# Routed experts of a mixture on their own tokens, by scatter and gather, instead of on all tokens

## Chip, cores and metric

One core of one Trainium2 chip. The metric is the time of one execution in device microseconds (us), as the median of several runs. A profile is one execution with the hardware profiler on.

## What is computed

Four residual layers on x of (2, 512, 256); each adds the layer norm of a block's output to x. The first three (a recurrent time mixing, an expert-choice layer, a delta-rule attention) are not touched by the change. The fourth is a mixture with a shared part and 8 routed experts of which each token takes 2:

```python
g = x @ sw1.T
u = x @ sw2.T
shared_out = jax.nn.silu(g) * u @ sw3.T            # 1024 hidden
scores = jax.nn.sigmoid(x @ router_w.T)            # 8 experts
_, top_idx = jax.lax.top_k(scores + expert_bias, TOPK)   # TOPK = 2
top_scores = jnp.take_along_axis(scores, top_idx, axis=-1)
top_scores = top_scores / (top_scores.sum(-1, keepdims=True) + 1e-09)
combine = jnp.zeros((T, E), x.dtype).at[jnp.arange(T)[:, None], flat_idx].add(flat_sc)
h12 = jnp.einsum('td,ehd->teh', flat_x, w12)       # 2 x 128 hidden per expert
h1, h2 = jnp.split(h12, 2, axis=-1)
out_e = jnp.einsum('teh,edh->ted', jax.nn.silu(h1) * h2, w3)
routed_out = jnp.einsum('ted,te->td', out_e, combine)
return shared_out + routed_out
```

## The kernel before

`sandwich` runs four stages one after the other, each a block in which the five engines have their own queues and meet through semaphores. The last is `expert_mixture`. Tokens are 1024 = 8 tiles of 128 (`NT`), 4 tiles to a batch (`TB`), a batch is 512 columns (`T`), and the 256 features are 2 chunks (`C`). The order of work on each engine is the order in which its function issues instructions; nothing moves them.

In the last stage the hidden units of the shared part (8 groups of 128, `SH`) and the 8 experts (128 hidden units each) are treated alike: 16 groups (`HID`), for each of 2 batches, so 32 steps (`STEPS`). Every expert is computed for every token and its hidden rows are scaled by the token's share for that expert, zero for those not chosen.

All products use operands split into a high and a low part (`HI`, `LO`), and three of the four products of parts (`PRODUCTS`). In step n TensorE does `up(n)`: for the gate and for the up weight 6 products of 512 columns (2 chunks x 3). ScalarE takes `silu(n)` of the gate, VectorE multiplies with the up half, GpSimd scales by the share where the group is an expert (L2243), ScalarE casts the high part (`high`, L2190), GpSimd subtracts for the low part (L2249), and three steps later (`LAG`) TensorE does `down(n)`: 12 products of 256 columns (L2135), which accumulate over the 16 groups in PSUM banks 0 and 1.

At the stage's head ScalarE and VectorE normalize x into xm, TensorE turns xm (L2090) into PSUM, the two engines split the turned rows (L2169, L2271) and ScalarE copies them once more (L2173) for the exact scores (L2098, after the first up product). VectorE chooses the two experts and makes the shares (`choose`, `weigh`) between the first steps, TensorE turns the shares (`turn_shares`, L2105), and they go to memory and back, spread over all partitions (L2220, L2226). The weights come turned from an earlier stage and are split, two groups of four 128 x 128 tiles per step, by ScalarE (`high_weights`, L2159) and VectorE (`low_weights`, L2262) in the first 14 steps. The first batch's sums are kept, normalized and added to x between the second batch's steps; the second batch's at the end (L2367, L296, L253, L2196, L2317), and x is stored (L2231).

```python
for n in range(STEPS + LAG):
    if n < STEPS:
        up(n)
    if n == SCORE_STEP:
        score()
    if n == SHARE_STEP:
        turn_shares()
    if n >= LAG:
        down(n - LAG)
```

## Time and profile before

| what | us |
|---|---|
| median of 3 runs (lowest, highest) | 476.74 (476.24, 477.44) |
| the profiled execution | 476.85 |
| its span, first to last instruction | 475.1 |
| TensorE busy in the span | 367.0 (77%) |
| VectorE, ScalarE, GpSimd busy | 294.2, 254.9, 122.4 |
| last stage, from its first instruction | 319.24 to 475.1 |

The difference between the execution's own time and its span, 1.75 us, lies before the first and after the last instruction. PE is TensorE's products, PEld its weight loads, which overlap them; DVE is VectorE, ACT ScalarE, POOL GpSimd, SP the queue that issues plain transfers. A q behind an engine's name is its queue (the sequencer). A duration of a TensorE product overlaps the next one's; how fast they follow one another is read from the chain or from the first and last of a run. The granted clock (PEclk) is a share of 2.4 GHz, 0.50 being 1.2 GHz.

### The profile page before, as it was taken

To read this page: it belongs to the slowest core of one execution; us is meant where nothing else is said; L and a number is where in the kernel's file an instruction comes from. 1 tells how busy PE (TensorE), PEld (TensorE's weight loads), DVE (VectorE), ACT (ScalarE), POOL (GpSimd) and SP (SyncE) were. 2 spreads that over 40 slices of the span, in tenths; PEclk is the share of its full clock that TensorE was granted. 3 is DMA by queue.
4 is the path that set the end of the run, shared out by engine and by line. 5 is a ranking of instruction groups with operands and counts; after the bars stand their busy time and mean duration, and the time that the engine had idled before them with its cause. 6 is when DMAs were issued, how large, how long until landed. Compare 5 with 4: busy or idle time off the path is not lost. (4 is left out here: it accounts for less than half of the span.)

```text
span 475.1 us, 10071 instructions
## 1 busy us (share of the span) xinstructions
PE 367.0 (77%) x4130; PEld 291.6 (61%) x4130; DVE 294.2 (62%) x622; ACT 254.9 (54%) x471; POOL 122.4 (26%) x148
## 2 busy tenths in 40 slices
PE   2999778866699766522158898846999999999993
PEld 1544567765477655311156455636888888888883
DVE  5799997796436565999973567784584211422223
ACT  2889774475457775582332457648745333354323
POOL 5393001400000015000017200030233665323661
PEclk9999989897999999555558959996899999999998
DMA  7790000000000000000000000000014500000001
GB/s 220 246 351 20 0 0 1 2 0 0 0 3 3 1 3 1 1 0 1 0 0 4 4 3 5 3 1 1 0 36 146 178 0 1 0 2 15 31 1 44
DMA packets 12489, 15.82 MB, mean 33 GB/s; under 512 B 2046, under 2 KB 10644, under 8 KB 12444
## 3 DMA queue, kind: packets, MB, share of 16 engines
q1 hardware_dynamic: 12444, 15.18, 10.2%
q8 instruction: 33, 0.54, 0.5%
q14 instruction: 12, 0.10, 0.1%
HBM read 14.09 MB, written 1.08 MB: 32 GB/s over the span
## 5 line engine op out<-in xcount | busy, mean ns | idle before, releaser
L2328 DVE TENSOR_TENSOR third<-third,ps 128x512 f32<-128x512 f32 x32 | 22.0, 686 | 81.7 <-PE ps L2119 67.7
L2249 POOL TENSOR_TENSOR hidden_r<-third,hidden_r 128x512 fp32r<-128x512 f32 x31 | 41.2, 1329 | 89.3 <-ACT hidden_r L2190 89.3
L2135 PEld LDWEIGHTS ps<-down_r,hidden_r 128*128 128x128 f32 x384 | 49.2, 188 | 3.2 <-POOL hidden_r L2249 0.9
L2135 PE MATMUL ps<-down_r,hidden_r 128*128 128x256 f32 x384 | 50.2, 280 | 0.7 <-POOL hidden_r L2249 0.7
L2119 PE MATMUL ps<-xm_r,gate_r 128*128 128x512 f32 x192 | 50.2, 398 | 0.0
L2190 ACT CAST hidden_r<-third 128x512 fp32r<-128x512 f32 x32 | 19.9, 623 | 56.4 <-PE ps L2135 56.4
L2119 PE MATMUL ps<-xm_r,up_r 128*128 128x512 f32 x192 | 50.0, 397 | 0.0
L2119 PEld LDWEIGHTS ps<-xm_r,up_r 128*128 128x128 f32 x192 | 36.9, 192 | 7.8
L1509 PE MATMUL ps<-ident,area 128*128 128x128 f32 x32 | 8.4, 414 | 40.4 <-DVE area L1839 40.4
L2119 PEld LDWEIGHTS ps<-xm_r,gate_r 128*128 128x128 f32 x192 | 34.8, 192 | 5.9 <-issue 0.2
L1509 PEld LDWEIGHTS ps<-ident,area 128*128 128x128 f32 x32 | 5.5, 207 | 43.2 <-DVE area L1839 43.2
L1836 DVE TENSOR_TENSOR third<-area 128x124 f32<-128x124 f32 (+15 forms) x31 | 29.2, 943 | 1.1
L2179 ACT ACTIVATE third<-ps 128x512 f32<-128x512 f32 x32 | 19.2, 599 | 19.4 <-PE ps L2119 19.4
L1839 DVE TENSOR_TENSOR area<-area,third 128x124 f32<-128x124 f32 (+15 forms) x31 | 27.9, 900 | 1.1
L1681 ACT ACTIVATE area<-ps,own_side 128x512 f32<-128x512 f32 (+1 forms) x16 | 15.9, 1100 | 19.9 <-PE ps L1509 19.9
L1737 ACT COPY area<-third 32x128 f32<-32x128 f32 x64 | 18.9, 295 | 14.0 <-DVE third L1883 12.7
L1130 POOL TENSOR_SCALAR keys_by_head<-k_t,own_fourth 128x512 f32<-128x512 f32 x4 | 3.9, 987 | 81.8 <-ACT k_t L1275 81.8
L1162 PE MATMUL ps<-w_r,x_r 128*128 128x512 f32 x96 | 19.2, 349 | 3.6 <-DVE beta_rows L1355 2.1
L2243 POOL TENSOR_TENSOR third<-third,stored 128x512 f32<-128x512 f32 x15 | 19.3, 1290 | 0.0
L1162 PEld LDWEIGHTS ps<-w_r,x_r 128*128 128x128 f32 x96 | 14.9, 188 | 7.0 <-issue 3.5
L1180 PE MATMUL ps<-proj_rows,third 128*32 128x128 f32 x384 | 15.2, 285 | 4.4 <-ACT qkv L1301 3.6
L1582 PE MATMUL ps<-area,k_t 128*32 128x128 f32 x128 | 15.5, 335 | 1.8 <-DVE area L1892 0.7
(343 smaller groups left out, 838.1 us busy)
## 6 DMA issues: line engine op xcount, KB each, us to landing
stored<-share_dram SPq DMA_DIRECT2D x8, 512.0 KB, 5.9
stored<-in_L_ffn_sw_dram SPq DMA_DIRECT2D x3, 1024.0 KB
stored<-in_L_ffn_w_dram SPq DMA_DIRECT2D x1, 2048.0 KB
x<-L_attn_hidden_state_dram SPq DMA_DIRECT2D x4, 256.0 KB, 3.4
out_dram<-x SPq DMA_DIRECT2D x4, 256.0 KB, 2.2
w_nat<-in_L_attn_Wk_dram SPq DMA_DIRECT2D x1, 256.0 KB, 2.7
w_nat<-in_L_attn_Wv_dram SPq DMA_DIRECT2D x1, 256.0 KB, 2.9
w_nat<-in_L_attn_Wr_dram SPq DMA_DIRECT2D x1, 256.0 KB, 4.1
```

The costliest lines, as they stand in the source:

```text
L1162: last = nc.tensor.matmul(ps[:, bank, 0:cols.stop - cols.start], own, w_r[:, wp, ci, cols], start=i == 0, stop=i == len(passes) - 1)
L1681: last = a(spread_rows(r, count, side), rows, ACT.Copy, scale=core.own_side[:, side:side + 1])
L1737: nc.scalar.copy(u_place[strand[q], n % U_SLOTS, :, q, :], u[strand[q], n % U_KEPT].rearrange("p (h e) -> p h e", h=HH)) \
L1836: link(V.tensor_tensor(part, rows.unsqueeze(3).to_broadcast([P, below, G, j + 1]), inv[:, j, :, 0:j + 1].unsqueeze(1).to_broadcast([P, bel ...
L1839: last = V.tensor_tensor(inv[:, j + 1:, :, 0:j + 1], inv[:, j + 1:, :, 0:j + 1], part, ALU.subtract)
L2119: last = nc.tensor.matmul(ps[:, bank + which, :], w[:, wp, c, a, :], xm_r[:, xp, c, b * T:(b + 1) * T], start=i == 0, stop=i == C * len(PR ...
L2135: last = nc.tensor.matmul(ps[:, t // 2, t % 2 * D:(t % 2 + 1) * D], hidden_r[:, n % 2, hp, t * P:(t + 1) * P], down_r[:, wp, a, :], start= ...
L2179: a(gated[:, n % 2, :], ps[:, 4 + 2 * (n % 2), :], ACT.Silu).then_inc(silu_ready, 1)
L2190: nc.scalar.copy(hidden_r[:, n % 2, HI, :], hidden[:, n % 4, :]).then_inc(hidden_hi, 1)
L2243: nc.gpsimd.tensor_tensor(hidden[:, n % 4, :], hidden[:, n % 4, :], share[:, a - SH, b * T:(b + 1) * T], ALU.mult) \
L2249: nc.gpsimd.tensor_tensor(hidden_r[:, n % 2, LO, :], hidden[:, n % 4, :], hidden_r[:, n % 2, HI, :], ALU.subtract).then_inc(hidden_lo, 1)
L2328: V.tensor_tensor(hidden[:, n % 4, :], gated[:, n % 2, :], ps[:, 4 + 2 * (n % 2) + 1, :], ALU.mult) \
```

## The change

The shared part keeps its steps (now 16: 8 groups x 2 batches). Each expert sees the tokens that chose it. The 2 x 1024 token rows are put, sorted by expert, into tiles of 128 rows of which each belongs to one expert; 23 tiles (`SLOTS`) hold every possible division. VectorE finds each row's place (`choose`, `place_tokens`), with sums over tokens by two small products (`count`). GpSimd scatters the rows of xm to their places in memory by 16 indirect transfers, SP loads the rows back tile by tile, and after 9 shared steps (`EARLY`) TensorE goes over the 23 tiles: it turns the rows, reads the tile's expert number into a register (`own_expert`), does the up products with weights addressed by it (6 of 256 columns), turns the product's rows, and does the down products (3 of 256 columns). ScalarE and VectorE split what is turned. The results are stored to memory, GpSimd gathers each token's two result rows by 16 indirect transfers into `found`, and VectorE adds them, times the token's shares, to the shared part's sums (`combine`). The seven other shared steps stand between the tiles and the end.

Further: the row buffer in memory is filled with input rows at the kernel's start (`fill_rows`), constants 8 to 23 are added, the turning of the input no longer waits for ScalarE's splits, splits of weights are dealt out to 9 steps, the low part of hidden rows is VectorE's (`low`), and the first batch's norm moves from between the steps to the tail.

```diff
+        self.rows_dram, self.results_dram = (self.nc.dram_tensor(name, ((2 * NT + E - 1) * P, D), F32, kind="Internal").ap()
+                                              for name in ("rows_dram", "results_dram"))
...
+    def fill_rows(self, sp, rows):
+
+        sp.wait_ge(self.f_in, self.f_in_total)
+        for start in range(0, self.rows_dram.shape[0], N):
+            some = min(N, self.rows_dram.shape[0] - start)
+            sp.dma_start(self.rows_dram[start:start + some, :], rows[0:some, :]).then_inc(self.f_in, 16)
+            self.rows_filled += 16
...
+        for e in range(24):
...
-    HID = SH + E
+    SLOTS = 2 * NT + E - 1
+    STEPS, EARLY, LAG = B * SH, 9, 3
+    ROW_PARTS = (0, 2, NT)
+    RESULT_PARTS = ((0, 8), (8, 16), (16, 20), (20, SLOTS))
...
+        routed_up = sb("routed_up", [P, 2, C, E, 2 * P], F32R)
+        routed_down = sb("routed_down", [P, 2, E, D], F32R)
...
+        AHEAD, PER_STEP = 8, (0, 2, 2, 2, 2, 2, 2, 2, 2)
...
+        COMBINED = {STEPS - 4: (0, 1), STEPS - 3: (2, 3), STEPS - 1: (4,)}
...
-                    pe.wait_ge(xm_kept, B * C)
                     for t in range(NT):
+                        if t == 0:
+                            pe.wait_ge(xm_kept, ROUTER + C)
+                        if t == TB:
+                            pe.wait_ge(xm_lo_kept, KEPT_LO)
...
+                def count():
+
+                    pe.wait_ge(routed, CHOSEN)
+                    for k, weights in enumerate((core.ones[:], upto_own)):
+                        last = nc.tensor.matmul(ps[:, 2, k * NT * E:(k + 1) * NT * E], weights,
+                                                flat(both), start=k == 0, stop=k == 1,
+                                                skip_group_check=True)
+                    last.then_inc(scores_done, 1)
...
+                def own_expert(j):
+                    expert[j] = nc.tensor.value_load(owner[0:1, j:j + 1], min_val=0, max_val=E - 1)
+
+                def turn_rows(j):
+                    if j in ROW_PARTS:
+                        pe.wait_ge(rows_in[ROW_PARTS.index(j)], 16)
+                    if j == 0:
+                        pe.wait_ge(routed, OWNED)
+                    if j >= 2:
+                        pe.wait_ge(xm_lo_kept, KEPT_LO + j - 1)
+                    for c in range(C):
+                        last = nc.tensor.transpose(ps[:, 2 + j % 2, c * P:(c + 1) * P], rows[:, j, c * P:(c + 1) * P],
+                                                   ident[:])
+                    last.then_inc(xm_turned, 1)
+
+                def up_routed(j):
+                    pe.wait_ge(xm_lo_kept, KEPT_LO + j + 1)
+                    pe.wait_ge(prod_ready, tile(j - 2) if j >= 2 else shared(EARLY - 2 + j))
+                    if j == 0:
+                        pe.wait_ge(*kept(groups[-1]))
+                    for i, (c, wp, xp) in enumerate((c, *parts) for c in range(C) for parts in PRODUCTS):
+                        last = nc.tensor.matmul(ps[:, 4 + j % 2, 0:2 * P], rows_t[j % 2][:, xp, c],
+                                                routed_up[:, wp, c, bass.DynSlice(expert[j], 1), :], start=i == 0,
+                                                stop=i == C * len(PRODUCTS) - 1)
+                    last.then_inc(up_done, 1)
+
+                def turn_hidden(j):
+                    pe.wait_ge(prod_ready, tile(j))
+                    if j:
+                        pe.wait_ge(hidden_lo, tile(j - 1))
+                    nc.tensor.transpose(ps[:, 6, 0:P], routed_hidden[:, j % 3], ident[:]).then_inc(scores_done, 1)
+
+                def down_routed(j):
+                    pe.wait_ge(hidden_lo, tile(j))
+                    if j:
+                        pe.wait_ge(rows_kept, j)
+                    for i, (wp, hp) in enumerate(PRODUCTS):
+                        last = nc.tensor.matmul(ps[:, 7, 0:D], routed_t[j % 2][:, hp],
+                                                routed_down[:, wp, bass.DynSlice(expert[j], 1), :], start=i == 0,
+                                                stop=i == len(PRODUCTS) - 1)
+                    last.then_inc(down_done, 1)
...
+                for n in range(EARLY):
+                    up(n)
+                    if n == 0:
+                        score()
+                    if n == COUNT_STEP:
+                        count()
+                    if n >= LAG:
+                        down(n - LAG)
+                for n in range(EARLY - LAG, EARLY - 1):
+                    down(n)
+                for j in range(SLOTS + 2):
+                    if j < SLOTS:
+                        turn_rows(j)
+                        own_expert(j)
+                    if 1 <= j <= SLOTS:
+                        up_routed(j - 1)
+                    if j == 2:
+                        down(EARLY - 1)
+                    if j >= 3:
+                        turn_hidden(j - 3)
+                    if j >= 4:
+                        down_routed(j - 4)
+                up(EARLY)
+                turn_hidden(SLOTS - 1)
+                down_routed(SLOTS - 2)
+                down_routed(SLOTS - 1)
+                for n in range(EARLY + 1, STEPS + LAG):
                     if n < STEPS:
                         up(n)
-                    if n == SCORE_STEP:
-                        score()
-                    if n == SHARE_STEP:
-                        turn_shares()
-                    if n >= LAG:
+                    if n - LAG >= EARLY:
                         down(n - LAG)
...
+                def high_rows(j):
+                    act.wait_ge(xm_turned, ROUTER + TURNED + j + 1)
+                    nc.scalar.copy(rows_t[j % 2][:, HI], ps[:, 2 + j % 2, 0:D].rearrange("p (c f) -> p c f", c=C)) \
+                        .then_inc(xm_hi_kept, 1)
+
+                def silu_routed(j):
+                    act.wait_ge(up_done, up_tile(j))
+                    a(gated[:, j % 2, 0:P], ps[:, 4 + j % 2, 0:P], ACT.Silu).then_inc(silu_ready, 1)
+
+                def high_routed(j):
+                    act.wait_ge(scores_done, HIDDEN_TURNED + j + 1)
+                    nc.scalar.copy(routed_t[j % 2][:, HI], ps[:, 6, 0:P]).then_inc(hidden_hi, 1)
+
+                def keep_rows(j):
+                    act.wait_ge(down_done, tile(j))
+                    nc.scalar.copy(rows[:, j], ps[:, 7, 0:D]).then_inc(rows_kept, 1)
...
-                sp.wait_ge(share_t_kept, 1)
-                sp.dma_start(core.share_dram, share_t).then_inc(share_out, 16)
-                sp.wait_ge(share_out, 16)
-                for part in range(2):
-
-                    sp.wait_ge(kept_dve, quad_kept[2 * part + 1])
-                    for e in range(4 * part, 4 * part + 4):
-                        sp.dma_start(share[:, e, :], core.share_dram[e].partition_broadcast(P)) \
-                            .then_inc(share_in[part], 16)
+                sp.wait_ge(rows_out, 16 * 2 * NT)
+                for part, start in enumerate(ROW_PARTS):
+                    stop = (ROW_PARTS + (SLOTS,))[part + 1]
+                    sp.wait_ge(*kept(quads[1][-1] if part < 2 else groups[-1]))
+                    sp.dma_start(rows[:, start:stop], tiles(core.rows_dram)[:, start:stop, :]) \
+                        .then_inc(rows_in[part], 16)
+
+                for start, stop in RESULT_PARTS:
+                    sp.wait_ge(rows_kept, stop)
+                    sp.dma_start(tiles(core.results_dram)[:, start:stop, :], rows[:, start:stop]) \
+                        .then_inc(results_out, 16)
...
+                pool.wait_ge(core.f_in, core.f_in_total + core.rows_filled)
+                pool.wait_ge(routed, PLACED)
+                for t in range(NT):
+                    for k in range(2):
+                        nc.gpsimd.indirect_dma_start(core.rows_dram, bass.IndirectOffsetOnAxis(slots[:, k, t:t + 1], 0),
+                                                     xm[:, t, :], None).then_inc(rows_out, 16)
+                pool.wait_ge(results_out, 16 * (1 + len(RESULT_PARTS)))
+                for t in range(NT):
+                    for k in range(2):
+                        nc.gpsimd.indirect_dma_start(found[:, k, t, :], None, core.results_dram,
+                                                     bass.IndirectOffsetOnAxis(slots[:, k, t:t + 1], 0)) \
+                            .then_inc(results_in[t // 2], 16)
...
+                def place_tokens():
+
+                    dve.wait_ge(scores_done, 2)
+                    link(V.tensor_tensor_scan(flat(upto_tile), flat(not_first[:]), ps[:, 2, 0:NT * E], 0.0, ALU.mult,
+                                              ALU.add))
...
+                    V.tensor_copy(slots[:], slots_f[:]).then_inc(routed, 1)
...
+                def low(n):
+                    dve.wait_ge(hidden_hi, shared(n))
+                    V.tensor_tensor(hidden_r[:, n % 2, LO, :], hidden[:, n % 4, :], hidden_r[:, n % 2, HI, :],
+                                    ALU.subtract).then_inc(hidden_lo, 1)
...
+                def combine(t):
+
+                    if t % 2 == 0:
+                        dve.wait_ge(results_in[t // 2], 16 * 4)
+                    if t < TB:
+                        link(V.scalar_tensor_tensor(y[:, t], found[:, 0, t], share[:, 0, t:t + 1], y[:, t], ALU.mult,
+                                                    ALU.add))
+                    else:
+                        link(V.tensor_scalar(y[:, t], found[:, 0, t], share[:, 0, t:t + 1], None, ALU.mult))
+                    return V.scalar_tensor_tensor(y[:, t], found[:, 1, t], share[:, 1, t:t + 1], y[:, t], ALU.mult,
+                                                  ALU.add)
...
+                for n in range(4, AHEAD):
+                    low_weights(n)
+                dve.wait_ge(scores_done, 1)
+                for n in range(EARLY):
+                    product(n)
+                    if n == 0:
+                        choose()
+                    if n == PLACE_STEP:
+                        place_tokens()
+                    if n:
+                        low(n - 1)
+                    for k in groups_of(n):
+                        low_weights(k)
+                    if n == WEIGH_STEP:
+                        weigh()
+                low(EARLY - 1)
+                for j in range(SLOTS + 3):
+                    if j < SLOTS:
+                        low_rows(j)
+                    if 1 <= j <= SLOTS:
+                        product_routed(j - 1)
+                    if j == 1:
+                        keep_first()
+                    if j == SLOTS + 2:
+                        product(EARLY)
+                    if j >= 3:
+                        low_routed(j - 3)
+                for n in range(EARLY + 1, STEPS):
+                    product(n)
+                    low(n - 1)
+                    for t in COMBINED.get(n, ()):
+                        last = combine(t)
+                    if n == STEPS - 2:
+                        link(last)
+                        finish_first(0)
+                low(STEPS - 1)
+                finish_first(1)
+                for t in range(STEPS_COMBINED, NT):
+                    last = combine(t)
+                    if t == STEPS_COMBINED:
+                        finish_first(2)
+                link(last)
                 for t in range(TB):
                     if t % 2 == 0:
-                        dve.wait_ge(down_done, STEPS + t // 2)
-                    last = V.bn_stats(norm.stats[:, TB + t, :], summed(t))
+                        dve.wait_ge(down_done, shared(STEPS - 1) + t // 2)
+                    link(V.tensor_tensor(y[:, TB + t], y[:, TB + t], summed(t), ALU.add))
+                    last = norm.tile_stats(y, TB + t)
```

TensorE, an inner tile of the routed part in the changed kernel (stored holds the token rows and, transposed next, the hidden rows; owner the experts' numbers):

```order
L2220 MATMUL ps<-ident,stored 128x128 [waits xm_lo_kept]
L2220 MATMUL ps<-ident,stored 128x128
L2210 TENSOR_LOAD owner
L2210 ISA x2
L2230 ISA [waits prod_ready,xm_lo_kept]
L2230 MATMUL ps<-routed_up,xm_r 128x256 x2
L2230 ISA
L2230 MATMUL ps<-routed_up,xm_r 128x256
L2239 MATMUL ps<-ident,stored 128x128 [waits hidden_lo,prod_ready]
L2246 REGISTER_ALU [waits routed_rows_kept,hidden_lo]
L2246 MATMUL ps<-routed_down,xm_r 128x256 x2
```

Nothing of this is in the kernel before, whose queue there goes from one `up` to one `down` of 12 products each; register instructions stand between the products, and the first of a group carries its waits.

GpSimd in the last stage before (hidden_r the split hidden rows; third holds the hidden rows themselves):

```order
L2249 TENSOR_TENSOR hidden_r<-third,hidden_r 128x512 [waits hidden_hi] x2
L2249 TENSOR_TENSOR hidden_r<-third,hidden_r 128x512 [waits down_done,hidden_hi] x6
L2243 TENSOR_TENSOR third<-third,stored 128x512 [waits prod_ready,share_in_first]
L2249 TENSOR_TENSOR hidden_r<-third,hidden_r 128x512 [waits down_done,hidden_hi]
L2243 TENSOR_TENSOR third<-third,stored 128x512 [waits prod_ready,share_in_first]
```

and in the changed kernel (stored now holds `found`):

```order
L2395 MEMSET third 128x128
L2396 AFFINE_SELECT third<-third 128x128 [waits masks_order]
L2403 DMA rows_dram<-xm,slots 2944x256 [waits tokens_routed,f_in,masks_order]
L2403 DMA rows_dram<-xm,slots 2944x256 x15
L2408 DMA stored<-results_dram,slots 128x256 [waits rows_in_2]
L2408 DMA stored<-results_dram,slots 128x256 x15
```

The subtractions and scalings have gone from GpSimd (the subtractions to VectorE), and 32 indirect transfers have come.

VectorE at the end of the changed kernel (xm holds the sums, stored the gathered rows):

```order
L2498 TENSOR_TENSOR hidden_r<-third,hidden_r 128x512 [waits hidden_hi]
L313 RECIPROCAL ln_inverse_std<-ln_std_dev 128x4 [waits ln_std]
L278 SCALAR_TENSOR_TENSOR ln_shift<-ln_mean_var,ln_inverse_std 128x4 [waits dve_order]
L2535 TENSOR_SCALAR xm<-stored,share 128x256
L2536 SCALAR_TENSOR_TENSOR xm<-stored,share,xm 128x256 [waits dve_order]
L2548 SCALAR_TENSOR_TENSOR x<-xm,ln_inverse_std,x 128x256 [waits scores_kept] x4
L2535 TENSOR_SCALAR xm<-stored,share 128x256 [waits results_in_3]
L2536 SCALAR_TENSOR_TENSOR xm<-stored,share,xm 128x256 [waits dve_order]
L2535 TENSOR_SCALAR xm<-stored,share 128x256
L2536 SCALAR_TENSOR_TENSOR xm<-stored,share,xm 128x256 [waits dve_order]
L2608 TENSOR_TENSOR xm<-xm,ps 128x256 [waits down_done,dve_order]
L302 BN_STATS ln_stats<-xm 128x6 [waits dve_order]
```

Before, the last subtraction was followed by the four statistics straight from PSUM; now the first batch's roots and adds, three pairs of combining and a sum ahead of each statistic stand there.

## Rows read from the trace of the kernel before

**Rows 1.** Head of the page: span, busy time by engine, bytes moved in 40 slices.

```profile
span 475.1 us, 10071 instructions
...
PE 367.0 (77%) x4130; PEld 291.6 (61%) x4130; DVE 294.2 (62%) x622; ACT 254.9 (54%) x471; POOL 122.4 (26%) x148
...
GB/s 220 246 351 20 0 0 1 2 0 0 0 3 3 1 3 1 1 0 1 0 0 4 4 3 5 3 1 1 0 36 146 178 0 1 0 2 15 31 1 44
```

**Rows 2.** Chain of waits that ended last, in time: start us, us, what.

```profile
320.02 2.07 ACT xm L272 x4
...
324.29 3.68 PE ps L2090 x16
327.96 3.39 PE ps L2119 x12
331.35 3.47 PE ps L2098 x32
...
348.89 0.97 PE ps L2105 x8
...
366.45 1.41 PE ps L2135 x12
367.86 2.73 PE ps L2119 x12
...
465.19 2.42 PE ps L2135 x18
467.62 0.02 issue
467.64 1.48 DVE ln_stats L2367 x4
...
470.84 1.68 DVE x L2317 x4
```

**Rows 3.** Stretches: us, busy PE, PEld, DVE, ACT, POOL, granted clock, DMA share, GB/s.

```profile
324.30:328.00 3.70, 3.70 (x17) 3.54 (x18) 2.45 (x5) 1.76 (x3) 0.00 (x0) 0.50 0.00 0
380.00:420.00 40.00, 40.00 (x231) 35.27 (x230) 9.20 (x21) 12.23 (x20) 19.08 (x15) 1.00 0.00 1
200.00:250.00 50.00, 16.39 (x275) 13.36 (x262) 45.34 (x48) 21.05 (x25) 1.80 (x3) 0.53 0.00 0
```

**Rows 4.** Timeline of TensorE, 68 to 76 us: turns of weight tiles.

```profile
72.17 2.78 PE L129 MATMUL ps<-ident,stored 128*128 128x128 f32 x24
```

**Rows 5.** Timeline of SP's queue, 0 to 60 us: issues of small transfers.

```profile
4.70 0.25 SPq L383 DMA_DIRECT2D vec_rows<-urrent_token_weight_dram  x1
...
12.91 3.71 SPq L166 DMA_DIRECT2D onorm<-in_L_attn_onorm_w_dram  x8
```

**Rows 6.** Groups by shape, 315 to 476 us: busy us, mean ns | idle before.

```profile
L2249 POOL TENSOR_TENSOR hidden_r<-third,hidden_r 128x512 fp32r<-128x512 f32 x31 | 41.2, 1329 | 89.3 <-ACT hidden_r L2190 89.3
...
L2190 ACT CAST hidden_r<-third 128x512 fp32r<-128x512 f32 x32 | 19.9, 623 | 56.4 <-PE ps L2135 56.4
...
L2262 DVE TENSOR_TENSOR down_r<-stored,down_r 128x512 fp32r<-128x512 f32 x8 | 5.4, 686 | 0.1
...
L2306 DVE COPY xm<-ps 128x256 f32<-128x256 f32 x4 | 1.4, 417 | 4.8 <-PE ps L2135 4.8
...
L2292 DVE TENSOR_TENSOR first<-first,scores 128x64 f32<-128x64 f32 x1 | 0.2, 226 | 0.0
```

**Rows 7.** Transfers: line, count, KB each, median us from issue to landing.

```profile
out_dram<-x SPq DMA_DIRECT2D x4, 256.0 KB, 2.2
...
onorm<-in_L_attn_onorm_w_dram SPq DMA_DIRECT2D x8, 0.1 KB, 2.6
```

**Rows 8.** Timeline of GpSimd, 0 to 130 us; in brackets idle before and releaser.

```profile
1.81 1.20 POOL L178 MEMSET numbers<- 128x1 f32 x8
...
18.48 1.86 POOL L199 TENSOR_SCALAR third<-third,conv_w 128x131 f32<-128x131 f32 x3 [9.59 <-DMA onorm<-in_L_attn_onorm_w_dram]
```

379 lines of the change are left out of this document (212 added, 167 removed).

## The prediction

> **What bounds the kernel now.** I read the head of the page first, then the chain of waits over the last stage, then that stage by stretches, and last the groups of instructions by shape. The span is 475.1 us of 476.85 us for the profiled execution; the median of the runs shown is 476.74, so the two may stand for one another. The changed stage is the last one, from about 319 us. Its chain consists almost entirely of TensorE [rows 2]: 12 products of 512 columns take 2.73 us and 12 of 256 take 1.41, so a step of up and down products costs 4.14 us, and there are 32 of them (2 batches of 16 groups). Between 380 and 420 us TensorE is busy without a gap at the full granted clock [rows 3]. VectorE, ScalarE and GpSimd wait for it there. So the time is TensorE's queue, and a change pays as far as it shortens that queue without putting a wait in it.
>
> **The change, part by part.** *Removed steps.* The 8 routed experts are no longer computed for every token: 16 of the 32 steps go. 16 x 4.14 = **-66.2 us** [rows 2], on the path entirely.
>
> *Added tiles.* 23 tiles of 128 token rows come instead. Each has 2 turns of its rows, 6 up products of 256 columns, 1 turn of its hidden rows and 3 down products of 256 columns. A product of 256 is 1.41/12 = 0.118 us [rows 2]; a turn at full clock 2.78/24 = 0.116 us [rows 4]. The array's share is 9 x 0.118 + 3 x 0.116 = 1.41 us. Besides, TensorE's queue has to read the tile's expert number from SBUF into a register (TENSOR_LOAD) and run eight register instructions, which the trace of before nowhere shows. Below: nothing, if the queue runs ahead of the array. Above: each of the nine at the shortest instruction which the trace shows a queue carrying out itself, a transfer's issue of 0.25 us [rows 5], which makes 1.41 + 2.25 = 3.66. The load is the one that reaches out to memory, so I price it like one of SP's small issues, 3.71/8 = 0.46 us [rows 5]. The register instructions touch nothing outside the queue; I take 0.02 us each, the gap that the chain of waits calls "issue" [rows 2], 0.16 together. Some of the load is behind waits on a semaphore, so I don't hide it: 2.03 us per tile, 23 x 2.03 = **+46.7 us** (32.4 to 84.2). The Trainium skill (DMA: Bandwidth & Descriptors, Latency and other measured facts) gives about 600 ns as the floor of a `tensor_load`; by that, as an estimate, a tile would be 2.17 and the sum 3.2 us higher. No run here shows it.
>
> The other engines of a tile fit under 2.03 us: ScalarE reads 256 columns twice and 128 twice. A 512-column cast takes 0.62 and VectorE's 256-column copy 0.42 [rows 6]; with 0.42 and 0.3, twice each, that is 1.44 us, and VectorE's three reads are 0.42 + 2 x 0.3 = 1.02. Within an iteration each turned bank is read before it is needed again one iteration later. Filling and draining this pipeline (first tile's turn, cast, subtraction; last tile's mirror image; the four copies of the first batch's sums on VectorE at the second tile) is some 0.12 + 0.42 + 0.42 at each end plus hand-overs: **+2.5 us** (1 to 5).
>
> *Head.* The turning of the input now starts when two rows of a batch are there instead of behind ScalarE's eight copies and splits: before, the turns run from 324.29 at 0.23 us each, at half clock, and the first up product at 327.96 [rows 2, 3]. Now they can start near 321.1, so the first batch is turned near 323, and with two casts, two subtractions and the first weights the product starts near 325.7. The scores hang on copies of the turned rows as before, so they end about 2.0 us earlier. The eight turns of the shares, 0.97 us [rows 2], go. New on the path: two small sums (count) that wait for VectorE's choice. Choice is a product (0.69) and 20 small instructions; they end about 3.9 us after the scores, while the up product between lasts about 3.7, so count costs about 0.6. Then 15 linked small instructions (0.23 each [rows 6]) stand on VectorE ahead of the third product, which comes about 0.4 us late. Sum: -2.0 - 0.97 + 0.6 + 0.4 = **-2.0 us** (-4 to +2). From then on VectorE has a product, a subtraction that was GpSimd's (1.33 there, 0.69 here [rows 6]) and two weight splits per step: 4 x 0.69 = 2.76, under the step's 4.14.
>
> *Scatter and gather.* GpSimd issues 16 indirect transfers of 128 rows, then 16 back. The trace has none. Below: 0.46 us each, SP's issue. Above: each waiting for the one ahead to land, 0.46 + 2.6 [rows 5, 7]. I take 1.33, what GpSimd's own 128-row instructions take [rows 6], for it is that engine which prepares them. Places known near 340.9, the first tile wanted near 368.7 (after 9 up and 8 down steps): 27.8 us, less a landing (2.6) and the load of the first two tiles (2.2 [rows 7]) leaves 23, so up to 1.43 us each costs nothing. On the way back the last pair is wanted 28 us after the last tile; less the store (2.6) and a landing (2.6), again 1.42 each. **0 us** at 1.33 (21.3), with the seven remaining shared steps as cover; without that cover it would be the whole 21.
>
> *Tail.* Before, from the last product's end to the span's end: 475.1 - 467.6 = 7.5 us [rows 1, 2]. Now VectorE has behind its last subtraction (about 1.8 us before the products end) the first batch's roots, one linked pair to combine, four adds (0.42 each at the spacing of [rows 2], 1.68/4), two more pairs (0.9 each), then four sums with a linked statistic (0.85 each) where there were four statistics alone (1.48). That puts the statistics' end about 6.9 us behind the products instead of 1.5: **+5.4 us** (2 to 8). The wait of 0.3 us net at the last down product of before goes: **-0.3**.
>
> Covered and free: 16 more constants on GpSimd's queue at 1.20/8 = 0.15 us, 2.4 in all, ahead of a wait of 9.59 us for a transfer [rows 8]; if that wait were gone they'd cost 2.4. Three fills of the row buffer (3 MB) on SP's queue behind the weights, when the transfers are idle from 40 us on [rows 1]; SP has nothing else until the last stage.
>
> Sum: -66.2 + 46.7 + 2.5 - 2.0 + 0 + 5.4 - 0.3 = -13.9. **476.85 - 13.9 = 463 us.** The tile's price breaks even at 2.03 + 13.9/23 = 2.63 us.
>
> **The rivals.**
> *A, GpSimd's transfers become the bound (slower).* If each of the 32 has to wait out one VectorE instruction of 0.69 us, it takes 2.02 us. Then the scatter is 16 x (2.02 - 1.43) = 9.4 us late at the first tile, and the gather 16 x (2.02 - 1.42) = 9.6 at the last pairs: 463 + 19 = 482. It decides against the change from 1.43 + 13.9/32 = 1.86 us each. For it: VectorE is two thirds busy where the scatter runs; against: no row shows GpSimd and VectorE holding each other up in this stage, its 1.28 to 1.33 hold throughout. The Trainium skill (SBUF — State Buffer, SBUF: two separate sides) says that VectorE in a two-port mode locks GpSimd out of the port through which it writes descriptors, so such a transfer waits for VectorE's instruction; nothing here shows it.
> *B, the clock falls in the tiles.* The granted clock is 0.50 while the input is turned after a pause, and 0.53 between 200 and 250 us, where TensorE is busy a third of the time [rows 3]. At 1.2 GHz a tile is 9 x 0.236 + 3 x 0.23 = 2.81 us: 463 + 23 x 0.78 = 481. For it: gaps in every tile; against: the array would still be busy 70%.
> *C, the queue runs ahead.* The loads lie wholly under the array's work, 1.41 us per tile: 463 - 14.3 = 449.
> That the change does not do what it says is no rival: the order of instructions shows the tiles and the loads.
>
> **How the numbers follow.** Forecast 0.53, A 0.20, B 0.10, C 0.17. About 0.3% (1.4 us) is what a measurement of this kernel can tell from no change. The forecast's own range is 455 to 474 (tile 1.7 to 2.5 us); a twentieth of all lies near break-even, and a part of the forecast goes over it through the load's upper bound: faster 0.66, same 0.05, slower 0.29. The range goes from C to beyond A and B: 447 to 486; the upper bound of nine full issues (500) is left out.
>
> **What would show it.** A tile's period in the routed part: 2.0 us says the load is paid, 1.4 that it is hidden, 2.8 with a granted clock of 0.5 says B. GpSimd's indirect transfers 1.3 us apart, and no wait of the first turned rows for their load, say the scatter is covered; a TensorE wait of some 10 us there says A. The statistics' end about 7 us behind the last product confirms the tail. I am wrong if a tile costs over 2.6 us at full clock, or if a transfer that no row of before shows stands between the shared steps and the tiles.

## The result: 475.5 us, a ratio of 0.991, where 463 us was forecast

The changed kernel takes 475.51 us (median of 20 runs, 470.23 to 489.35), the kernel before 477.76 us beside it (20 runs, 474.8 to 484.5). The ratio is 0.9906 with a 95% interval of 0.9881 to 0.9931: faster by about 1%. The forecast was faster by 2.9% (463.0 of 476.74 us). So the sign was right and the time lies in the range of 447 to 486, but only about a third of the gain that was worked out came (0.94% of 2.9%). The profiled execution took 470.29 us, its span 468.2 us; it is one of the fastest. Medians here and below count every execution, while ratios leave out those in a slower state that some executions of every kernel fall into.

The head of the page of the changed kernel, beside [rows 1], with the software queue that the indirect transfers use:

```profile
span 468.2 us, 10194 instructions
...
PE 345.0 (74%) x4018; PEld 270.8 (58%) x4018; DVE 322.6 (69%) x730; ACT 256.0 (55%) x527; POOL 101.4 (22%) x152
...
PEclk9999989897999997755559959997899789999986
...
q0 software_dynamic: 1536, 4.20, 2.8%
```

TensorE has 22 us less work than in [rows 1], and the span is 6.9 us shorter. The other 15 us have become time in which TensorE stands. TensorE's timeline shows where (start, busy time, line, operation, output and inputs, count, in brackets the idle time ahead and what ended it; the lines chosen are the landmarks of the last stage):

```profile
325.88 1.66 PE L2182 MATMUL ps<-xm_r,gate_r 128*128 128x512 f32 x6 [0.35 <-DVE xm_r L2430]
...
363.96 0.60 PE L2198 MATMUL ps<-down_r,hidden_r 128*128 128x256 f32 x3 [0.42 <-issue]
366.07 0.40 PE L2198 MATMUL ps<-down_r,hidden_r 128*128 128x256 f32 x2 [1.51 <-issue]
366.80 0.52 PE L2198 MATMUL ps<-down_r,hidden_r 128*128 128x256 f32 x1 [0.33 <-issue]
367.50 1.45 PE L2198 MATMUL ps<-down_r,hidden_r 128*128 128x256 f32 x6 [0.18 <-issue]
369.38 5.03 PE L2198 MATMUL ps<-down_r,hidden_r 128*128 128x256 f32 x24 [0.44 <-DVE hidden_r L2498]
374.26 0.60 PE L2220 MATMUL ps<-ident,stored 128*128 128x128 f32 x4
...
420.67 1.62 PE L2182 MATMUL ps<-xm_r,gate_r 128*128 128x512 f32 x6
...
453.17 5.49 PE L2198 MATMUL ps<-down_r,hidden_r 128*128 128x256 f32 x24 [3.39 <-DVE hidden_r L2498]
```

The first up product comes 2.1 us earlier than in [rows 2] (325.88, not 327.96), as forecast. Then one down product, 12 matmuls with no wait between them, takes from 363.96 to 368.95 us where it took 1.41 [rows 2], and "issue" says that the profile shows nothing which TensorE waited for. The next two products take 5.03 us where two of 1.41 are 2.82, and the first turned rows (L2220) come at 374.26, not at 368.7 as worked out. Ahead of the last two down products TensorE stands 3.39 us, and they take 5.49. ScalarE's timeline, and behind it some lines of VectorE's, show that these two stood as well:

```profile
353.89 0.60 ACT L2309 ACTIVATE third<-ps 128x512 f32<-128x512 f32 x1 [0.71 <-PE ps L2182]
354.39 1.13 ACT L2288 CAST routed_up<-stored 128x512 fp32r<-128x512 f32 x2
360.48 0.62 ACT L2315 CAST hidden_r<-third 128x512 fp32r<-128x512 f32 x1 [4.97 <-remote]
363.97 0.60 ACT L2309 ACTIVATE third<-ps 128x512 f32<-128x512 f32 x1 [2.87 <-PE ps L2182]
...
367.99 0.62 ACT L2315 CAST hidden_r<-third 128x512 fp32r<-128x512 f32 x1 [2.39 <-remote]
...
445.93 0.62 ACT L2315 CAST hidden_r<-third 128x512 fp32r<-128x512 f32 x1 [3.85 <-remote]
448.71 0.60 ACT L2309 ACTIVATE third<-ps 128x512 f32<-128x512 f32 x1 [2.16 <-remote]
451.78 1.22 ACT L2315 CAST hidden_r<-third 128x512 fp32r<-128x512 f32 x2 [2.47 <-remote]
```

```profile
361.14 0.69 DVE L2498 TENSOR_TENSOR hidden_r<-third,hidden_r 128x512 fp32r<-128x512 f32 x1 [3.39 <-ACT hidden_r L2315]
...
367.58 0.69 DVE L2493 TENSOR_TENSOR third<-third,ps 128x512 f32<-128x512 f32 x1 [4.55 <-issue]
...
451.65 0.69 DVE L2493 TENSOR_TENSOR third<-third,ps 128x512 f32<-128x512 f32 x1 [2.65 <-issue]
```

"remote" is a releaser that the profile doesn't know. The cast at 360.48 waits for a down product whose 12 matmuls began at 355.05 and ended near 356.5; the activation at 363.97 for 6 matmuls that began at 356.47 and ended near 357.9. Both come 4 to 6 us after what they wait for, and only part of it is handed on from one to the next: the cast had ended at 361.10. VectorE's products at 367.58 and 451.65 had stood 4.55 and 2.65 us, put down to "issue". All this falls while GpSimd issues the scatter (341.42 to 365.8 us) and the gather (428.58 to 449.9), each time in their last third, and ends 1.7 us after the last issue.

Which engine is late, these views do not print. But the trace also records when each engine's semaphore was counted up; with such an increment an engine tells the others that an instruction is done. Throughout the last stage, every increment of ScalarE and VectorE that is recorded comes within 0.02 us of its instruction's end. TensorE's do so too, except here (steps are counted from 0; the gate and the up half of an up product are 6 matmuls each):

| product of TensorE | its end, us | its increment, us | what started then |
|---|---|---|---|
| down 3 | 356.63 | 360.41 | ScalarE's cast, 360.48 |
| gate half of up 7 | 358.02 | 363.95 | ScalarE's activation, 363.97 |
| up half of up 7 | 359.38 | 367.50 | VectorE's product, 367.58 |
| a down product at the gather | 444.22 | 445.85 | ScalarE's cast, 445.93 |
| up half of the last up product there | 446.96 | 451.57 | VectorE's product, 451.65 |

So ScalarE and VectorE are not held up themselves. They wait for word from TensorE, which comes up to 8.1 us late, and two of TensorE's own pauses at the down product end with the same increments (363.95 and 367.50). The ends of TensorE's products are worked out by the profiler. But four increments within 0.28 us (367.50 to 367.78), for groups of products that take 1.4 us each, suggest that the products had been done before and only the word of it was held back.

GpSimd itself keeps its pace:

```profile
341.42 2.79 POOL L2403 DMA_INDIRECT rows_dram<-xm,slots  x1 [21.00 <-DVE owner L2477]
344.51 1.87 POOL L2403 DMA_INDIRECT rows_dram<-xm,slots  x1 [0.30 <-issue]
346.69 2.08 POOL L2403 DMA_INDIRECT rows_dram<-xm,slots  x1 [0.30 <-issue]
349.08 0.96 POOL L2403 DMA_INDIRECT rows_dram<-xm,slots  x1 [0.30 <-issue]
...
364.83 0.96 POOL L2403 DMA_INDIRECT rows_dram<-xm,slots  x1 [0.30 <-issue]
```

The granted clock follows the standstill (stretches: length, busy time of PE, PEld, DVE, ACT, POOL, granted clock, DMA share, GB/s):

```profile
363.00:369.00 6.00, 3.51 (x15) 2.49 (x13) 1.08 (x3) 2.63 (x6) 2.18 (x3) 0.82 0.26 80
369.00:375.00 6.00, 5.47 (x28) 5.23 (x28) 3.94 (x7) 1.98 (x6) 0.00 (x0) 0.61 0.63 192
375.00:382.00 7.00, 4.83 (x29) 4.57 (x29) 3.50 (x10) 1.76 (x6) 0.00 (x0) 0.76 0.76 256
382.00:420.00 38.00, 33.97 (x248) 29.33 (x246) 18.70 (x62) 22.15 (x82) 0.00 (x0) 1.00 0.16 56
452.00:460.00 8.00, 5.49 (x24) 5.19 (x24) 7.54 (x20) 4.28 (x8) 0.00 (x0) 0.57 0.20 68
```

At 1.00 (2.4 GHz) the tiles run undisturbed; behind each standstill the mean is near 0.6, a mixture of the two levels.

To compare runs I cut the last stage at TensorE's landmarks: **A** from the first up product to the first turned rows, **B** from there to the next shared up product (the tiles), **C** from there to the span's end. In the changed kernel that is A 374.26 - 325.88 = 48.38, B 46.41, C 468.2 - 420.67 = 47.53 us, together 142.32.

### The profile page after: what moved, and what is told of

Read it like the earlier page. It is cut to its first block and busy times, and to the rows that moved or that the text cites. A ratio compares the mean times of both kernels' runs of the same rounds, so it can differ in the third digit from the quotient of the medians.

```text
span 468.2 us, 10194 instructions
## 1 busy us (share of the span) xinstructions
PE 345.0 (74%) x4018; PEld 270.8 (58%) x4018; DVE 322.6 (69%) x730; ACT 256.0 (55%) x527; POOL 101.4 (22%) x152
## 5 line engine op out<-in xcount | busy, mean ns | idle before, releaser
L2198 PE MATMUL ps<-down_r,hidden_r 128*128 128x256 f32 x192 | 30.8, 320 | 6.7 <-DVE hidden_r L2498 3.8
L2198 PEld LDWEIGHTS ps<-down_r,hidden_r 128*128 128x128 f32 x192 | 29.4, 226 | 8.8 <-DVE hidden_r L2498 4.3
L2408 POOL DMA_INDIRECT stored<-results_dram,slots x16 | 16.7, 1045 | 67.4 <-DMA results_dram<-stored 62.8
L2230 PE MATMUL ps<-routed_up,xm_r 128*128 x138 | 23.4, 307 | 5.6 <-DVE stored L2510 2.7
L2182 PE MATMUL ps<-xm_r,gate_r 128*128 128x512 f32 x96 | 26.0, 407 | 1.0 <-ACT stored L2332 0.7
L2403 POOL DMA_INDIRECT rows_dram<-xm,slots x16 | 19.8, 1238 | 25.6 <-DVE owner L2477 21.0
L2182 PE MATMUL ps<-xm_r,up_r 128*128 128x512 f32 x96 | 25.2, 399 | 0.0
L2230 PEld LDWEIGHTS ps<-routed_up,xm_r 128*128 128x128 f32 x138 | 18.7, 198 | 10.2 <-issue 10.2
L2182 PEld LDWEIGHTS ps<-xm_r,up_r 128*128 128x128 f32 x96 | 18.8, 195 | 4.2
L2182 PEld LDWEIGHTS ps<-xm_r,gate_r 128*128 128x128 f32 x96 | 17.6, 193 | 4.7 <-issue 0.8
```

Of the source, the lines that this page charges most:

```text
L2182: last = nc.tensor.matmul(ps[:, bank + which, :], w[:, wp, c, a, :], xm_r[:, xp, c, b * T:(b + 1) * T], start=i == 0, stop=i == C * len(PR ...
L2198: last = nc.tensor.matmul(ps[:, t // 2, t % 2 * D:(t % 2 + 1) * D], hidden_r[:, n % 2, hp, t * P:(t + 1) * P], down_r[:, wp, a, :], start= ...
L2230: last = nc.tensor.matmul(ps[:, 4 + j % 2, 0:2 * P], rows_t[j % 2][:, xp, c], routed_up[:, wp, c, bass.DynSlice(expert[j], 1), :], start=i ...
L2403: nc.gpsimd.indirect_dma_start(core.rows_dram, bass.IndirectOffsetOnAxis(slots[:, k, t:t + 1], 0), xm[:, t, :], None).then_inc(rows_out, 16)
L2408: nc.gpsimd.indirect_dma_start(found[:, k, t, :], None, core.results_dram, bass.IndirectOffsetOnAxis(slots[:, k, t:t + 1], 0)) \
```

## Experiments

Theory S: the indirect transfers in flight hold up all the engines (more exactly, by the increments above, TensorE's word to them). Theory K makes it narrower: the transfers pile something up, and the trouble begins after some 12 in a row. The rivals were chance (N), the bytes (B), each transfer by its share (P), and the addresses in memory.

### Leaving the scatter, the gather, or both out; plain transfers in their place

Scatter left out, with the waits for its landing, which this cut does not show (the gather likewise; "neither" is both):

```
-                        nc.gpsimd.indirect_dma_start(core.rows_dram, bass.IndirectOffsetOnAxis(slots[:, k, t:t + 1], 0),
-                                                     xm[:, t, :], None).then_inc(rows_out, 16)
```

Plain, in the scatter (the gather likewise):

```
-                        nc.gpsimd.indirect_dma_start(core.rows_dram, bass.IndirectOffsetOnAxis(slots[:, k, t:t + 1], 0),
-                                                     xm[:, t, :], None).then_inc(rows_out, 16)
+                        nc.gpsimd.dma_start(tiles(core.rows_dram)[:, 2 * t + k, :], xm[:, t, :]).then_inc(rows_out, 16)
```

> Leaves out the scatter: the 16 indirect transfers that put the tokens' rows into expert order are not issued, so the tiles compute on the rows that fill the buffer. Theory S (the 16 indirect transfers, while in flight, hold up all engines, and the clock falls after): the late instructions at 357 to 369 us go, down product 5 takes 1.4 us and not 5, the first turned rows come at about 368 us and not 374, and the profiled run falls from 470.3 to about 464; the stall at 445 to 452 us stays. Rival N (the stall is chance, or belongs to the shared step itself with its splits of weights): the late instructions stay and the time falls by at most 1 to 2 us, the wait for the rows.

> Leaves out the gather: the 16 indirect transfers that fetch each token's two results are not issued and the sums take what lies in that memory. Theory S: the stall of 3.4 us ahead of the last down products and their 2.5 us at half clock go, the profiled run falls from 470.3 to about 465; the stall at 357 to 369 us stays. Rival N: under 2 us, since the sums never waited for the gather for long.

> Leaves out both scatter and gather. Theory S: both stalls go, about 458 to 460 us, and the runs lie close together as they did before the change (within about 1 per cent), since what spreads them is the stalls. Rival N: 467 to 469, with the spread of the changed kernel (4 per cent).

> The 32 indirect transfers become plain transfers of GpSimd with the same tiles and the same bytes, to and from fixed places, so that the rows no longer lie by expert. Theory S (it is the indirect kind): no stall, about 460 us. Rival B (it is the bytes or the small packets in flight, whatever the kind): stalls at the same places, about 470 us, as the changed kernel.

| kernel | median us | ratio to before, 95% | A | B | C |
|---|---|---|---|---|---|
| changed | 475.51 | 0.991 (0.988 to 0.993) | 48.38 | 46.41 | 47.53 |
| no scatter | 473.92 | 0.986 (0.981 to 0.991) | 42.80 | 46.55 | 53.33 |
| no gather | 470.33 | 0.982 (0.978 to 0.987) | 48.50 | 47.04 | 45.28 |
| neither | 463.14 | 0.969 (0.964 to 0.973) | 42.07 | 45.97 | 45.32 |
| plain | 461.78 | 0.967 (0.962 to 0.971) | 42.53 | 46.55 | 45.33 |

Each part loses its own stall and keeps the other's. A falls by 5.6 to 6.3 us without the scatter (until the third up product, ahead of the stall, the kernels of this table lie within 0.8 us, 11.13 to 11.86); C falls by 2.25 without the gather. Both kernels came out slower than S had them (474.22 and 470.64 us in the profiled executions, not 464 and 465), and the time of the first alone, 1.6 us less in the median, would fit chance as well; it is the late instructions, gone in one place and kept in the other, that speak for S. Without the gather, TensorE's part of C is 5.5 us shorter (32.50 us to the last down product's end, not 37.99), but VectorE had used the standstill for sums that now stand behind TensorE, and 3.2 us come back. Without the scatter, the stall at the gather was larger, 8.0 us (53.33 against 45.32): its size differs between the profiles (C is 51.56 with the constant expert below). With neither, the late instructions are gone. Its runs lie between 460.5 and 466.0 us, near the 1 per cent that S had; but the plain kernel, which does not stall either, has 461.0 to 472.3, so the spread decides nothing. With neither, TensorE's landmarks read:

```profile
326.44 1.66 PE L2182 MATMUL ps<-xm_r,gate_r 128*128 128x512 f32 x6 [0.35 <-DVE xm_r L2421]
...
368.51 0.60 PE L2220 MATMUL ps<-ident,stored 128*128 128x128 f32 x4
...
440.59 6.42 PE L2198 MATMUL ps<-down_r,hidden_r 128*128 128x256 f32 x48
```

The plain transfers decide between the kind and the bytes. In the stretch of the scatter the queue moves the same packets and bytes in both kernels; the line is the same from 340 to 367 us of the changed kernel and from 340 to 368 us of the plain one (packets, MB, share of the 16 DMA engines):

```profile
q0 software_dynamic: 768, 2.10, 21.7%
```

GpSimd issues the 16 plain ones in 8.73 us, nearly three times as fast as the indirect ones (24.4), and nothing stalls: no increment of TensorE is over 0.02 us late, with neither and with plain transfers. So it is neither the bytes nor the queue. Nor do data queue up in the changed kernel: the trace's packets of 14 of the 16 transfers of the scatter are moved within 0.53 us each, and done before those of the next one begin. The whole of both places is worth 9.0 us in the profiled executions (142.32 - 133.36) and 2.2% by the ratios (0.991 - 0.969), that is 10.4 us. The rest of the kernel varies too. The plain kernel's profiled execution, for one, reaches its first up product 10 us later than the changed kernel's, with the clock down in a stage that the change does not touch. Here the stretch of the changed kernel, then of the plain one:

```profile
280.00:300.00 20.00, 18.70 (x604) 11.66 (x600) 15.06 (x41) 14.29 (x43) 0.00 (x0) 0.96 0.02 4
```

```profile
280.00:300.00 20.00, 19.84 (x513) 12.51 (x512) 12.93 (x36) 12.12 (x37) 0.00 (x0) 0.50 0.01 4
```

That is why I compare A, B and C and not spans.

### Four in flight at most; half as many; a constant expert; ten steps ahead

The first edit is a wait for landing after every fourth transfer:

```
                                                      xm[:, t, :], None).then_inc(rows_out, 16)
+                    pool.wait_ge(rows_out, 32 * (t + 1)) if t % 2 else None
```

(the gather likewise). The second, *half*, is `for k in range(1)` in place of `range(2)`, with the counts of the waits halved. The third is

```
-                    expert[j] = nc.tensor.value_load(owner[0:1, j:j + 1], min_val=0, max_val=E - 1)
+                    expert[j] = j // 3
```

with plain slices where the register was used. The fourth is `EARLY` 10 and not 9, with the copies of the first batch's sums moved ahead of the tiles. Theory H, a rival on the constant expert, has the load of the expert's number hidden beside another wait.

> The changed kernel, but GpSimd waits after every fourth indirect transfer until those issued so far have landed, in the scatter and in the gather, so that never more than four are in flight. Theory K (the stalls come of what the transfers pile up: in both places the first late instruction came some 12 transfers after the first): the late instructions at 357 to 369 and 442 to 453 us go, and with them the clock falls; the scatter ends about 5 us later (three landings of some 1.5 us more), so the rows come about 4 us after down product 7: about 464. Rival P (every indirect transfer stops the other engines by its share, piled up or not): the stalls stay as long and the later scatter comes on top, 474 or more.

> Leaves out the second choice of every token in scatter and gather: 8 indirect transfers in each place and not 16. Theory K (pile-up, first late after some 12): no stall in either place, about 461 to 463, as with neither. Rival P (each transfer by its share): half of the 12 us that both cost, about 468.

> The expert of a tile is a constant of the program (tile number over three): TensorE's load of the number into a register and the addresses worked out from it go from all 23 tiles; the wrong experts' weights are used for some tiles. The prediction's tile term (0.46 us for the load and 0.16 for the register instructions, in the row): 14 us less than the changed kernel. Rival H (the load lies beside the wait for VectorE's product, which would end the tile anyway): under 4 us less.

> Ten shared steps ahead of the tiles and not nine, the copies of the first batch's sums ahead of the tiles: the rows have 4 us more to land before they are wanted. Theory S: the stall of all engines stays, as does the clock fall, but the 256, 768 and 1920 KB of rows land behind the tenth step, so the stutter at 374 to 382 us goes, 2 to 4 us less. Rival: nothing gained, since TensorE was held by its own down products and not by the rows.

| kernel | median us | ratio, 95% | A | B | C |
|---|---|---|---|---|---|
| wait after every 4 | 474.0 | 0.987 (0.974 to 0.999) | 48.86 | 47.02 | 48.40 |
| half | 462.6 | 0.962 (0.951 to 0.973) | 42.06 | 45.92 | 45.27 |
| constant expert | 467.43 | 0.972 (0.963 to 0.981) | 48.47 | 37.22 | 51.56 |
| ten steps ahead | 476.11 | 0.993 (0.988 to 0.999) | 53.57 | 45.01 | 48.08 |

*Half* has A and C of "neither": eight in a row cost nothing, so the stall is no share per transfer, and P falls. *Waits after every four*: hardly a late instruction is left (one of TensorE's increments is 0.80 us late, the others 0.26 at most). But GpSimd's waits put the end of the scatter off, and the time comes back as a plain wait of TensorE for the rows, 6.66 us, with the granted clock down behind it (0.64 from 375 to 382 us):

```profile
374.38 0.69 PE L2220 MATMUL ps<-ident,stored 128*128 128x128 f32 x2 [6.66 <-DMA stored<-rows_dram]
```

So the mechanism was as K said and the time was not: I had the wait for the rows at 4 us, forgot the clock, and the gather, put off too, made the end 3.1 us longer (48.40 against 45.32).

*The constant expert* prices the tile's load on the path: B falls from 46.41 to 37.22, by 9.19 us, 0.40 us for each of 23 tiles. The prediction had 0.46 + 0.16, which makes 14.3 us. So 5.1 us of that did not come, but it is far more than the 4 of rival H.

*Ten steps*: A grows by 5.2 us and not by the 4.14 of a step, since the stall stays and TensorE now also waits 1.60 us for VectorE's copies. B falls by 1.4. C keeps the stall of the gather with one step less ahead of it, 48.08, although the program there is a step shorter. The rival was right: TensorE was held by its own late products and not by the rows, for in both kernels the first turned rows follow the last product ahead of them without a wait.

### One wait; a slower pace; the list in order; ten steps again

One wait for landing after the eighth transfer, in the scatter and in the gather (with nine steps ahead and with ten); or, without any wait for landing,

```
                                                      xm[:, t, :], None).then_inc(rows_out, 16)
+                        link(nc.gpsimd.memset(core.same_head[:], 0.0))
```

(the gather likewise); or the changed kernel with a list made by GpSimd, `nc.gpsimd.iota(own, pattern=[[P, 2 * NT]], base=0, channel_multiplier=1)`, in place of `slots`.

> The changed kernel with one wait for landing, after the eighth of the sixteen indirect transfers, in the scatter and in the gather. Theory K (the other engines stop only once more than about 12 were issued without such a wait): no late instructions in either place. The scatter then ends 1.4 us later, TensorE waits some 3.5 us for the rows (42.1 us from the first up product to the rows without a scatter, 45.6 with this one), the part after the tiles takes 32.7 us and not 38.0: 138 us from the first up product to the end of the program, and not 142.3; median about 471. Rival: the stalls come back in the second eight, 475.

> The changed kernel with a small memset of GpSimd (128 x 128, 0.2 us in the trace) after each indirect transfer and no wait for landing: a slower pace. If the pace is what piles up, the stalls go as with the waits of four, about 472 to 474. If it is that GpSimd never waits for what it issued, the first late instruction comes again after some 12 transfers: 475 or more.

> One wait for landing after the eighth transfer, and ten shared steps ahead of the tiles and not nine: the tenth step's 4.16 us cover the wait for the rows. From the first up product: 46.8 us to the rows, 45 to 46 for the tiles, 28.5 after them, and 15.5 at the end since the gather is covered by one step less: 136 us, median about 469, the fastest that computes what the reference asks for. Rival: the gather's end decides, and what is won ahead of the tiles is lost behind them: 471 to 472, as with nine steps.

> The 32 indirect transfers stay indirect, but the list of rows is that of the plain transfers (row 128 times the transfer's number plus the partition), so that rows no longer lie by expert. If the indirect kind of instruction is what stops the engines, stalls as in the changed kernel and 475; if it is the scattered addresses in memory, no stalls and 462, as with plain transfers.

| kernel | median us | ratio, 95% | A | B | C |
|---|---|---|---|---|---|
| one wait after 8 | 471.65 | 0.987 (0.983 to 0.991) | 46.28 | 47.35 | 47.00 |
| memset between | 470.05 | 0.981 (0.977 to 0.985) | 48.30 | 47.38 | 45.32 |
| ten steps, one wait | 469.72 | 0.980 (0.977 to 0.984) | 49.30 | 46.67 | 45.52 |
| list in order | 471.81 | 0.985 (0.982 to 0.988) | 49.02 | 46.52 | 47.58 |

*The memset* settles pace against waiting: GpSimd never waits for a landing, takes 0.2 us more per transfer (where nothing else slows it, 1.46 us from one to the next in the scatter and 1.44 in the gather, not 1.26 and 1.25), and the late instructions are gone in both places: no increment of TensorE is over 0.02 us late. Whether it is the longer pace or GpSimd's own instruction in between that helps, no run here separates. C is that of "neither", 45.32. Here is GpSimd's timeline, and then TensorE's with what is left, the wait for the rows:

```profile
357.05 0.97 POOL L2403 DMA_INDIRECT rows_dram<-xm,slots  x1 [0.28 <-POOL same_head L2405]
358.02 0.22 POOL L2405 MEMSET same_head<- 128x128 f32 x1
358.51 0.97 POOL L2403 DMA_INDIRECT rows_dram<-xm,slots  x1 [0.28 <-issue]
```

```profile
379.60 0.69 PE L2220 MATMUL ps<-ident,stored 128*128 128x128 f32 x2 [5.54 <-DMA stored<-rows_dram]
```

*One wait* is enough in the scatter (A 46.28, TensorE waits 4.04 us for the rows), but in the gather one late cast (2.57 us, "remote") remains. *The list in order* keeps both stalls (A 49.02, C 47.58, ScalarE's "remote" waits of 2.2 to 4.5 us): the scattered addresses are not the cause, the indirect kind is. Its median is lower than expected, 471.81 and not 475, about the spread of such kernels. *Ten steps, one wait* met its median (469 expected), but not its stretches, 141.5 us and not 136: A is 49.30 and not 46.8, with 1.60 us of waiting for VectorE's copies ahead of the rows and the second up product at a granted clock of 0.50 (its halves take 2.91 and 2.76 us, where 1.52 is usual).

### The bytes of the indirect transfers; both places paced

Only the first 16 elements of each row (`xm[:, t, 0:16]`, into the buffer seen as rows of 16; `found[:, k, t, 0:16]` back). And, with the work whole, one wait in the scatter and the memsets in the gather, with nine steps ahead; and the same with ten, the copies moved ahead as before, and

```
-        COMBINED = {STEPS - 4: (0, 1), STEPS - 3: (2, 3), STEPS - 1: (4,)}
+        COMBINED = {STEPS - 3: (0, 1), STEPS - 2: (2, 3), STEPS - 1: (4,)}
```

> The changed kernel, but each of the 32 indirect transfers moves only the first 16 elements of a row (64 bytes and not 1024), to a packed part of the memory: the rest of a row is left out, so the tiles compute on the fill and the sums on old memory. If it is the instructions with their 128 row addresses each that pile up, the stalls stay: 475 or more. If it is the bytes that they move on top of their addresses, no stalls: 462 to 464.

> Nine shared steps ahead of the tiles as in the changed kernel, a wait for landing after the eighth transfer of the scatter, a memset after each transfer of the gather. Theory K: no stall in either place, 46.3 us to the rows (as with one wait in both places), 32.5 us after the tiles and 12.8 at the end (as with the spaced transfers): 139 us, median about 469, against 471.65 where the gather too had one wait only.

> Ten shared steps ahead of the tiles, a wait for landing after the eighth transfer of the scatter, a memset after each transfer of the gather, and the sums of the first tokens one step later (13, 14 and 15 and not 12, 13 and 15), so that VectorE meets the gather's landings one step later too. Theory K: no stall; from the first up product 49.3 us to the rows and 46.7 for the tiles, as with ten steps before, then 29 to 30 us to TensorE's end and not 33.05, and 13 to 15 at the end: 139 us in all, median about 467. Rival: the sums that wait move to the end of the program, and the part behind TensorE's end grows by what the part before it lost: 469 to 470.

| kernel | median us | ratio, 95% | A | B | C |
|---|---|---|---|---|---|
| small rows | 474.74 | 0.992 (0.988 to 0.995) | 48.59 | 46.45 | 47.62 |
| nine steps, paced | 470.84 | 0.981 (0.977 to 0.986) | 47.76 | 46.90 | 45.28 |
| ten steps, paced | 467.28 | 0.976 (0.971 to 0.981) | 48.14 | 45.15 | 43.87 |

A sixteenth of the bytes leaves A and C as in the changed kernel, within 0.3 us. The queue moves 0.12 MB in the scatter, ScalarE stands as before, and TensorE's increments come up to 8.1 us late again:

```profile
q0 software_dynamic: 480, 0.12, 2.1%
```

```profile
362.69 0.62 ACT L2315 CAST hidden_r<-third 128x512 fp32r<-128x512 f32 x1 [4.96 <-remote]
366.19 0.60 ACT L2309 ACTIVATE third<-ps 128x512 f32<-128x512 f32 x1 [2.88 <-remote]
```

So it is the indirect instructions themselves, in close succession, that hold TensorE's word back, not their data. The kernel with ten steps and both places paced is faster than before and than the change: 467.28 us, 0.976 of before. It still waits:

```profile
376.08 0.60 PE L2220 MATMUL ps<-ident,stored 128*128 128x128 f32 x4
...
448.64 4.62 PE L2198 MATMUL ps<-down_r,hidden_r 128*128 128x256 f32 x24 [2.50 <-DVE hidden_r L2500]
```

The first turned rows no longer wait for their load. What is left ahead of them is 1.60 us for the copies of the first batch's sums, which VectorE may only make when the scatter has landed, and behind the tiles 2.50 us for VectorE's sums, which wait for the gather. TensorE's part of C took 32.03 us and not the 29 to 30 expected, the end 11.84 and not 13 to 15; the median lies within 0.3 us of what was expected. The kernel with nine steps has A 47.76 and not the 46.3 expected, with its second up product at 0.50 too (2.91 and 2.76 us), and a median of 470.84 and not 469.

## Why the prediction was right in its sign and wrong in its size

*The step that failed* is "Scatter and gather", **0 us** at 1.33 us each "with the seven remaining shared steps as cover". The price of a transfer was nearly right: 0.96 and 0.30 of issue, 1.26 us in the scatter from the fourth on, and 1.33 in the mean in the gather. But the step asked only whether GpSimd would be done in time, and took the engines of the cover as undisturbed. They are not: after ten to twelve indirect transfers in a row TensorE's increments come 1.6 to 8.1 us late, the engines that wait for them stand, TensorE stands with them, and the granted clock falls behind the standstill. In place of 0 the runs show 9.0 us in the profiled executions and 10.4 by the ratios. With neither transfer the kernel takes 0.969 of the time before, with plain ones 0.967, and the forecast was 0.971 (463.0 of 476.85): the rest of the sum, taken together, held, in part by errors that cancel (see the tile below).

*Also short in that step*: the first three transfers take 2.79, 1.87 and 2.08 us, so that the scatter's mean is 24.4/16 = 1.52 us and over the limit of 1.43. In the changed kernel this lies under the stall; where the stall is taken away, it is part of TensorE's wait for the rows (5.54 us with the memsets, of which these make 16 x 0.2 = 3.2 themselves; so some 2.3 us, by this estimate, are the scatter's own).

*The tile*: 2.03 us forecast, 46.7 for 23 and 2.5 for filling and draining, 49.2. From the first turned rows to the last tile's down product it is 425.4 - 374.26 = 51.1 us, of which down product 8 (1.41) and an up product (2.73) are not tiles: 47.0. The load's part was mis-sized, 0.40 us on the path and not 0.62, 5.1 us too much for 23; the wait for VectorE's product of a tile (0.2 to 0.7 us ahead of 8 up products, 2.7 in all), which the working did not have, makes up for half of it. The sentence on the Trainium skill (DMA: Bandwidth & Descriptors, Latency and other measured facts) gave about 600 ns as the floor of such a load. The trace does not agree, and the measurement decides: the 23 loads take 0.30 us at the least and in the middle (by line: count, ns of the shortest, the middle and the longest one, first and last start):

```profile
L2210 PEldq TENSOR_LOAD <-owner x23: 297/305/887, 372.0 to 415.3; - x23
```

*The removed steps* came as worked out, 16 are gone, and so did the start of *the head*: the first up product is at 325.88 us (forecast 325.7). *The tail* was forecast at 7.5 + 5.4 = 12.9 us from the last product's end to the span's; with neither transfer it is 459.8 - 447.0 = 12.8.

*Rival A* (GpSimd waits out VectorE, 2.02 us each, 482) named the right place and the wrong engine: GpSimd was hardly slowed, TensorE was. By the Trainium skill (SBUF — State Buffer, SBUF: two separate sides) VectorE can lock GpSimd out of the port through which it writes descriptors. From the fourth transfer on the trace shows nothing of it: 0.96 us beside a VectorE that is busy 3.23 of 4 us (348 to 352); whether VectorE's instructions there are of the kind that locks, no row tells. The first three are slow while it is busy 3.86 of 4 us (340 to 344) and 4.00 of 4 (344 to 348), which would fit; no run here separates that from a start-up cost. In the gather the first takes 0.98, with VectorE busy 1.43 of 4 us. *Rival B* did not come in the tiles, whose clock is 1.00 from 382 to 420 us, but a clock near 0.6 came behind the stalls. Its sum was too low as well: 2.81 us is the products alone at half clock, and with the 0.62 that the forecast adds for the load a tile would have been 3.43, the time 495. *Rival C* (loads hidden, 449) did not come: the constant expert shows that the loads are paid.

What stays open is what holds TensorE's increments back. The runs exclude the bytes (64-byte rows stall as well), the queue and its packets (plain transfers do not stall), the addresses (the list in order stalls) and a fixed share per transfer (eight are free). The loading of code does not fit either: no packet of an instruction queue is under way from 354.2 to 369.3 us. That 0.2 us more per transfer is enough suggests that something drains at about that pace. One trace of it may be that increments are missing from the record wherever indirect transfers run: of the scatter's 256 landing increments 81 are recorded in the changed kernel, 188 with the memsets and all 256 with plain transfers. So what is short may be the way that increments and their records take. Whether the recording itself has a part in the stall, no run here tells.

## What to carry to other kernels

Where several engines stand at once and the profile names no cause, look which engine's increments come late: the others may only be waiting for it. When work moves to an engine that seems free, ask not only whether it is done in time but also what it does to the engines beside it; a transfer of a kind that the trace lacks needs a rival of its own for that. Indirect transfers in a long row are to be paced: a 0.2 us memset between them, or a wait for landing after eight, took the stalls away here (all but one late cast of 2.57 us, with the wait) at the price of a later end, so such a row wants slack ahead of its reader. Compare kernels by stretches between landmarks where an earlier stage spreads the runs by more than the effect.
